# A two-layer graph network on one Trainium2 core: the f2 row sent in 4-byte pieces, set-up in finer steps, new step lists

## The chip, the cores and the metric

The kernel runs on 1 core of one Trainium2 chip. The metric is the device time in microseconds (us) of one execution. The engines are named as the profile names them: PE (TensorE matmuls), PEld (its weight loads), DVE (VectorE), ACT (ScalarE), POOL (GpSimd), SP (SyncE, which only issues DMAs). Each works through its own instruction list in order; lists meet at semaphores.

## The reference

The input x has 16 batch entries of 512 nodes with 256 features; adj is one 512 x 512 matrix of 0 and 1, the same for all entries. Cut to what matters:

```
h   = relu(layernorm(x))
# four attention heads, each with its own W (256x256) and a (2x256)
Wh  = h @ W;  f1 = Wh @ a[:256];  f2 = Wh @ a[256:]
e   = leaky_relu(f1[:, None] + f2[None, :], 0.01);  e = where(adj > 0, e, -1e9)
head = elu(softmax(e) @ Wh)
# a fifth head ("BACK") over the four heads side by side (1024 -> 256), then
y   = relu(out @ w1 + b1) @ w2 + b2 + out
x   = x + layernorm(y) * gamma + beta
h   = relu(layernorm(x))
x   = x + deg * (h @ Wi.T + b) + adj @ (h @ Wj.T)
```

For every head the score matrix needs f1 as one number per row and f2 as one number per column. f2 comes out of the product with one value per partition and has to be laid along the free axis of all 128 partitions.

## The kernel before, in words

Products that need precision are made of three matmuls on a split of each operand into a high and a low part (`product`, L775 to L785): ACT writes the high part, DVE the low part. The 512 nodes are 4 tiles of 128 (NC = 4). A batch entry has 10 **units**: a head times a half u of the rows (two tiles). Units 0 and 1 are head 0, 2 and 3 head 1, 4 and 5 the BACK head of an entry, 6 to 9 heads 2 and 3.

A unit goes through these steps, each on one engine: `rowmax` (DVE, L665: f2bc + mask, and its row maximum), `rowmath` (DVE, L679), `args` (ACT, L470: Prelu with f1 as bias, then Exp with the row sum), `rinv` and `scale` (DVE, L693 and L697), `turn_p` (PE, L844: 8 transposes), `probs` (ACT L482, DVE L688: high and low part), `attend` (PE, L854: 24 matmuls), `elu_neg`, `elu_exp` (ACT), `elu_out` (DVE), `hx` (ACT) and `hx_lo` (POOL). Around them stand per entry `norm_in`, `turn_in`, eight `m1` (12 matmuls each), four `mix2` (the BACK head's product, 24 matmuls each), `turn_out`, `ffn1`, `ffn2`, `norm_ff`, `x2`, `norm_gc`, `turn_gc`, two `conv_in`, `conv` and the store.

**The order of the work.** Each engine has a list of (step, index, late), `SP_STEPS` to `POOL_STEPS`. `steps` (L277) goes round the list; in round t it does the step for entry t - late, if there is one. So entries overlap: the attention of one entry, the feed-forward part of the one before and the convolution of the one before that run in one round. Steps named in `ONCE` (L275) are done for the first entry alone: they are set-up. An engine never skips a step that waits.

**PSUM** is four pairs of banks (`pairs`). PE's steps take them strictly in turn (L287 to L297): a PE step first waits until the pair's last user has been read (`take`, `lend`).

**How f2 gets to all partitions before.** `m1` ends on DVE with a copy of 4 columns out of PSUM (L663), f1 and f2 of two tiles; the BACK head's is in DVE's `mix2` (L718). Then PE's `f2turn` (L831) transposes the 128 x 4 column block into PSUM, ACT's `f2turn` (L463) copies the 4 x 128 result to `f2row`, SP's `f2send` (L337) writes it as 4 runs of 512 bytes to a row in DRAM scratch, and SP's `f2bcast` (L345) reads that row into all 128 partitions of one of two `f2bc` buffers. `rowmax` waits for it. It happens 5 times an entry, 80 times in all.

**Set-up before.** SP issues x of entry 0, then the head weights, a_heads, adj, W_gc, w1, w2 and the small vectors (L319 to L330). DVE starts with `norm_in` of entry 0 (L630), `wh_prep` of head 0 (L562), and `turn_in` (L654), and then alternates. `mask_` (L578) handles all four tiles at once, with a reduce on DVE. `load_wo` on SP (L361) brings W_out, a_out, b_gc and b2 in once `s_pick` and `s_wh` are there, since they go into buffers that set-up frees. `wo_prep` on DVE (L596) is one block of 5 + 16 + 3 operations. `adj_cast` (L617) and `adj_turn` (L623) are DVE's.

The opening of two lists, with entry numbers as b0, b1:

```
PE  turn_in.b0 m1(0,0) m1(0,1) m1(1,0) f2turn0 m1(1,1) gc_turn f2turn1 m1(2,0) m1(2,1)
    turn_p0 m1(3,0) turn_p1 attend0 m1(3,1) turn_p2 f2turn2 attend1 turn_in.b1 ...
DVE norm_in.b0 norm_in_out wh_prep0 turn_in.b0 wh_prep1 m1(0,0) wh_prep2 m1(0,1) mask m1(1,0)
    wh_prep3 m1(1,1) norm_in.b1 rowmax0 rowmath0 gc_turn rowmax1 rowmath1 rinv0 norm_in_out.b1
    scale0 m1(2,0) rowmax2 rowmath2 rowmax3 rinv1 m1(2,1) scale1 probs0 rowmath3 wo_prep ...
```

Of the kernel before, what the change touches and what calls it, by code (L numbers as in the profile page):

```python
# [21 lines left out]
ACT_STEPS = [
    ("hx", 0, 3), ("probs", 2, 3), ("f2turn", 2, 3), ("elu_neg", 1, 3), ("elu_exp", 1, 3), ("turn_in", 0, 2),
    ("turn_gc", 0, 5), ("args", 4, 4), ("elu_neg", 2, 3), ("elu_exp", 2, 3), ("f2turn", 3, 3), ("probs", 3, 3),
    ("args", 5, 4), ("conv_in", 0, 5), ("probs", 4, 4), ("hx", 1, 3), ("m1", (0, 0), 2), ("args", 6, 3), ("hx", 2, 3),
    ("conv_in", 1, 5), ("m1", (0, 1), 2), ("wh_prep", 0, 0), ("elu_neg", 3, 3), ("elu_exp", 3, 3), ("probs", 5, 4),
    ("elu_neg", 4, 4), ("wh_prep", 2, 1), ("elu_exp", 4, 4), ("probs", 6, 3), ("hx", 3, 3), ("m1", (1, 0), 2),
    ("args", 7, 3), ("f2turn", 0, 2), ("elu_neg", 5, 4), ("elu_exp", 5, 4), ("args", 8, 3), ("elu_neg", 6, 3),
    ("elu_exp", 6, 3), ("turn_out", 0, 4), ("probs", 7, 3), ("hx", 6, 3), ("m1", (1, 1), 2), ("probs", 8, 3), ("args", 9, 3),
    ("ffn1", 0, 4), ("elu_neg", 7, 3), ("elu_exp", 7, 3), ("hx", 7, 3), ("elu_neg", 8, 3), ("gc_turn", 0, 2),  # L30
    ("elu_exp", 8, 3), ("probs", 9, 3), ("f2turn", 1, 2), ("args", 0, 2), ("m1", (2, 0), 2), ("hx", 8, 3), ("args", 1, 2),
    ("elu_neg", 9, 3), ("elu_exp", 9, 3), ("m1", (2, 1), 2), ("probs", 0, 2), ("hx", 9, 3), ("wo_prep", 0, 2),
    ("norm_ff_out", 0, 4), ("norm_in_out", 0, 1), ("args", 2, 2), ("mix2", 0, 3), ("args", 3, 2), ("mix2", 1, 3),
    ("m1", (3, 0), 2), ("f2turn", -1, 3), ("probs", 1, 2), ("wh_prep", 1, 0), ("norm_gc_out", 0, 4), ("elu_neg", 0, 2),
    ("elu_exp", 0, 2), ("m1", (3, 1), 2), ("wh_prep", 3, 1),
]
# [945 lines left out]
```

## Time and profile before

| what | value |
|---|---|
| median of 3 runs | 1413.06 us (1412.38 to 1413.7) |
| the profiled execution's own time | 1413.76 us |
| its span in the trace | 1412.0 us |
| mean granted TensorE clock | 0.981 |
| PE busy | 1318.9 us, 93% of the span |
| DVE, ACT busy | 1097.5 us (78%), 1109.4 us (79%) |
| POOL busy | 346.7 us (25%) |

A busy share is the time in which an engine had an instruction running; starts of matmuls on PE lie closer together than their durations, because they are pipelined, so what a PE step takes is read from the distance of starts. The granted clock is TensorE's: 1.0 is 2.4 GHz, 0.5 is 1.2 GHz. The profiled execution is 0.7 us above the median.

### The profile page before, as it was taken

What the parts mean: (1) busy time and instruction counts of PE and PEld (TensorE: products, weight loads), DVE (VectorE), ACT (ScalarE), POOL (GpSimd) and SP (SyncE); (2) the same over time, 40 slices, a digit from 0 to 9 for tenths busy, and PEclk for the clock granted to TensorE, in tenths of its full rate; (3) what the DMA queues carried; (4) which work ended last, traced back from release to release, by engine and by line L of the source; (5) the groups of instructions that cost most, each with busy time, mean ns of one, the idle gap of its engine ahead of it and who ended that gap; (6) DMA issues with size and microseconds to landing.
All of it is one profiled execution on the core that took longest, in us unless ns stands there. A gap on an engine that the chain in (4) does not pass through costs nothing.

```text
span 1412.0 us, 27480 instructions
## 1 busy us (share of the span) xinstructions
PE 1318.9 (93%) x10024; PEld 1248.7 (88%) x10024; DVE 1097.5 (78%) x2841; ACT 1109.4 (79%) x2123; POOL 346.7 (25%) x234
## 2 busy tenths in 40 slices
PE   3689999999999999999999999999999999999874
PEld 3689898999999899999989999998999999899763
DVE  6997888787878878787887878788787878778442
ACT  3688987888888788887878878788887878888531
POOL 0021322314122231412223141222314122231411
PEclk9799999999999999999999999999999999999997
DMA  4211001011110101111020111102001110101000
...
DMA packets 42741, 55.14 MB, mean 39 GB/s; under 512 B 2864, under 2 KB 30832, under 8 KB 42480
## 3 DMA queue, kind: packets, MB, share of 16 engines
...
q14 instruction: 52, 0.43, 0.1%
...
## 4 chain that ended last, share of the span: by engine, by line
PE 66%; DVE 17%; ACT 11%; issue 6%; DMA 1%; POOL 0%; POOLq 0%; SPq 0%; ACTq 0%
PE ps L781 45%; PE ps L850 6%; PE ps L950 5%; PE ps L914 4%; PE ps L902 4%; DVE arg L701 3%; DVE arg L675 3%; ACT arg L479 2%; ACT elu L499 2%; DVE prob_lo L652 2%; DVE xb L742 2%; ACT arg L475 1%; DVE h2T_lo L652 1%; DVE zneg L683 1%; ACT prob_hi L485 1%
## 5 line engine op out<-in xcount | busy, mean ns | idle before, releaser
L398 POOL TENSOR_TENSOR hx_lo<-elu,hx_hi 128x512 fp32r<-128x512 f32 x128 | 177.3, 1385 | 867.2 <-ACT hx_hi L508 867.2
L781 PE MATMUL ps<-prob_hi,whx_hi 128*128 128x256 f32 x1024 | 301.6, 295 | 3.6 <-DVE prob_lo L652 3.6
L781 PE MATMUL ps<-prob_hi,whx_lo 128*128 128x256 f32 x1024 | 291.2, 284 | 0.0
L781 PE MATMUL ps<-prob_lo,whx_hi 128*128 128x256 f32 x1024 | 291.0, 284 | 0.0
L499 ACT ACTIVATE elu<-ps 128x512 f32<-128x512 f32 x160 | 94.4, 590 | 174.3 <-PE ps L781 174.3
L479 ACT ACTIVATE arg<-arg,nmax 128x512 f32<-128x512 f32 x320 | 226.6, 711 | 3.9 <-DVE nmax L686 3.8
L475 ACT ACTIVATE arg<-arg,fcol 128x512 f32<-128x512 f32 x320 | 211.9, 712 | 3.1 <-DVE gmax L675 3.1
L675 DVE CUSTOM_DVE_ANT_0 arg<-f2bc,mask 128x512 f32<-128x512 f32 x320 | 207.2, 684 | 5.4 <-DMA f2bc<-f_rows 5.4
L652 DVE TENSOR_TENSOR prob_lo<-ps,prob_hi 128x1024 fp32r<-128x1024 f32 x160 | 195.1, 1219 | 19.4 <-ACT prob_hi L485 17.8
L781 PEld LDWEIGHTS ps<-prob_hi,whx_hi 128*128 128x128 f32 x1024 | 197.5, 193 | 10.6 <-issue 5.9
L781 PEld LDWEIGHTS ps<-prob_hi,whx_lo 128*128 128x128 f32 x1024 | 197.6, 193 | 3.7 <-issue 3.6
L781 PEld LDWEIGHTS ps<-prob_lo,whx_hi 128*128 128x128 f32 x1024 | 197.6, 193 | 0.0
L850 PE MATMUL ps<-ident,arg 128*128 128x128 f32 x1280 | 167.3, 274 | 13.5 <-DVE arg L701 11.9
L711 DVE SCALAR_TENSOR_TENSOR elu<-elu,ps 128x512 f32<-128x512 f32 x128 | 87.7, 685 | 113.7 <-ACT elu L503 111.3
L701 DVE TENSOR_SCALAR arg<-arg,rinv 128x512 f32<-128x512 f32 x320 | 164.6, 556 | 2.4
L485 ACT ACTIVATE prob_hi<-ps 128x1024 fp32r<-128x1024 f32 x160 | 162.0, 1012 | 1.4 <-PE ps L850 1.4
L850 PEld LDWEIGHTS ps<-ident,arg 128*128 128x128 f32 x1280 | 144.8, 142 | 16.0 <-DVE arg L701 13.6
L781 PE MATMUL ps<-wh_hi,hT_hi 128*128 128x258 f32 x512 | 153.3, 299 | 2.5 <-DVE hT_lo L652 2.5
L781 PE MATMUL ps<-wh_lo,hT_hi 128*128 128x258 f32 x512 | 146.3, 286 | 0.0
L781 PE MATMUL ps<-wo_hi,hx_hi 128*128 128x258 f32 x512 | 146.0, 285 | 0.0
L781 PE MATMUL ps<-wh_hi,hT_lo 128*128 128x258 f32 x512 | 145.9, 285 | 0.0
L781 PE MATMUL ps<-wo_lo,hx_hi 128*128 128x258 f32 x512 | 144.9, 283 | 0.0
...
## 6 DMA issues: line engine op xcount, KB each, us to landing
f2bc<-f_rows SPq DMA_DIRECT2D x80, 256.0 KB, 3.2
...
f_rows<-f2row SPq DMA_DIRECT2D x80, 2.0 KB
...
```

Source lines behind the costliest of these rows:

```text
L398: pool.tensor_tensor(out=hx[1][:, 2 * c.h:2 * c.h + 2, c.u * HN:(c.u + 1) * HN], in0=elu[:, c.buf, :, :], in1=hx[0][:, 2 * c.h:2 * c.h + 2 ...
L475: act.activation(a[:, n, :], a[:, n, :], ACT.Prelu, bias=f1[:, n:n + 1], alpha=SLOPE).then_inc(arg_lin, 1)
L479: i = act.activation(a[:, n, :], a[:, n, :], ACT.Exp, bias=nmax[:, c.abuf, n:n + 1], accum_out=rsum[:, c.abuf, n:n + 1])
L485: act.activation(prob[0][:, c.buf, :, :].rearrange("p j i -> p (j i)"), pairs[c.pair][:, :, :].rearrange("p a n -> p (a n)"), ACT.Copy).th ...
L499: act.activation(elu[:, c.buf, :, :], pairs[c.pair][:, :, 0:F], ACT.Relu, scale=-1.0).then_inc(elu_neg, 1)
L652: return dve.tensor_tensor(out=dst, in0=src, in1=hi.bitcast(fp32), op=ALU.subtract)
L675: dve.tensor_tensor_reduce(out=arg[:, c.abuf, n, :], in0=f2bc[:, head % F2S, :], in1=mask[:, 2 * c.u + n, :], scale=1.0, scalar=-3.0e38, o ...
L701: i = dve.tensor_scalar(arg[:, c.abuf, n, :], arg[:, c.abuf, n, :], rinv[:, c.abuf, n:n + 1], None, ALU.mult)
L711: dve.scalar_tensor_tensor(out=dst, in0=elu[:, c.buf, :, :], scalar=-1.0, in1=pairs[c.pair][:, :, 0:F], op0=ALU.add, op1=ALU.max).then_inc ...
L781: i = pe.matmul(out, a, b_, start=(k == 0), stop=(k == n - 1))
L850: i = pe.transpose(p[:, j, n, :], arg[:, c.abuf, n, j * P:(j + 1) * P], ident[:, :])
L950: i = pe.matmul(pairs[c.pair][:, n // 2, (n % 2) * F:(n % 2 + 1) * F], adjT[:, j, n * P:(n + 1) * P], mj, start=(j == 0 and s == 0), stop= ...
```

## The change

f2 goes straight from its columns to the scratch row: `f2send` now reads the 128 x 4 column block and writes each element to its place, 512 pieces of 4 bytes. PE's and ACT's `f2turn` and the buffer `f2row` are gone.

```diff
             def f2send(c):
-                head = unit_number[c.b, c.info, 0] // 2
-                sp.wait_ge(f2_row, head + 1)
+                h = c.info
+                head = unit_number[c.b, h, 0] // 2
+                if h == BACK:
+                    sp.wait_ge(m2_read, 2 * (c.b + 1))
+                    column = fcol2[:, 1, :]
+                else:
+                    sp.wait_ge(m1_read, 2 * H * c.b + 2 * h + 2)
+                    column = fcol[:, h, 1, :]
                 if head >= 4:
                     sp.wait_ge(f2_spread[(head - 4) % F2S], 16 * ((head - 4) // F2S + 1))
-                sp.dma_start(f2_rows[head % 4].rearrange("(c q) -> c q", c=NC), f2row[:, :]).then_inc(f2_out[head % 4], 16)
+                sp.dma_start(f2_rows[head % 4].rearrange("(c q) -> q c", c=NC), column, allow_slow_non_contiguous=True).then_inc(f2_out[head % 4], 16)
...
-            def f2row_(c):
-                head = unit_number[c.b, c.info, 0] // 2
-                act.wait_ge(f2_turned, head + 1)
...
-            def f2turn(c):
...
-                take(c.pair)
-                pe.transpose(pairs[c.pair][0:NC, 0, 0:P], column, ident[:, :]).then_inc(f2_turned, 1)
-                lend((c.pair,), (f2_row, head + 1))
```

Set-up is cut finer. `wh_prep` on DVE leaves the low part of the weights to a step `wh_low`. `mask` works on two tiles at a time; its row sums move to ACT (`mask_` there, with accumulate), and a step `mask_end` finishes them. `adj_cast` (with the sums for deg) and `adj_turn` move from DVE to ACT. The b_gc part of `wo_prep` becomes `brow`; the rest becomes eight steps, one for each 128 rows of W_out:

```diff
+            def wh_low(c):
+                h = c.info
+                dve.wait_ge(s_wh_hi, h + 1)
+                for k in range(KC):
+                    i = dve.tensor_tensor(out=wh[1][:, k, h, 0:F], in0=w_heads[k][:, h, :], in1=wh[0][:, k, h, 0:F].bitcast(fp32), op=ALU.subtract)
+                i.then_inc(s_wh_lo, 1)
...
+            def mask_end(c):
+                dve.wait_ge(s_counted, c.info + 1)
...
+                i.then_inc(s_mask[c.info], 1)
+                if c.info == 0:
+                    dve.wait_ge(s_const, 3)
+                    dve.tensor_copy(pick[:, :], pick_st).then_inc(s_pick, 1)
...
+            def wo_prep(c):
+                k = c.info
                 for l in (LD_WO, LD_AO):
                     dve.wait_ge(ld[l], 16)
                 dve.wait_ge(s_gc_turned, 1)
...
+                for z in range(2):
+                    i = dve.tensor_tensor_reduce(out=xb[:, 2 * (k % 2) + z, :], in0=w_o[:, k, :], in1=a_o[:, z, :], scale=1.0, scalar=0.0,
+                                                 op0=ALU.mult, op1=ALU.add, accum_out=wsum2[:, k, z:z + 1])
+                link(i)
                 dve.wait_ge(s_wo_hi, 1)
+                link(dve.tensor_copy(wo[0][:, k, F:FA], wsum2[:, k, :]))
+                dve.tensor_tensor(out=wo[1][:, k, F:FA], ...)
+                dve.tensor_tensor(out=wo[1][:, k, 0:F], ...).then_inc(s_wo, 1)
...
             def load_wo(c):
                 sp.wait_ge(s_pick, 1)
+                sp.wait_ge(s_wh_lo, H)
                 sp.wait_ge(s_wh, H)
...
             def load_adj(c):
-                sp.wait_ge(s_wo, 1)
+                sp.wait_ge(s_wo, OC)
```

All five step lists are new, with `late` values up to 8. One round of three of them in the middle of the run, from `attend` of unit 5 on (numbers are units; b is the entry of heads 0 to 3, others are earlier ones):

```
PE  attend5 turn_p7 attend6 turn_p8 turn_out m1(2,0) attend7 ffn1 m1(2,1) turn_p9 attend8 m1(3,0)
    attend9 ffn2 mix2_0 mix2_1 turn_p0 mix2_2 mix2_3 turn_p1 m1(3,1) turn_in attend0 turn_p2
    attend1 turn_p3 turn_gc m1(0,0) attend2 m1(0,1) conv_in0 conv_in1 turn_p4 attend3 conv
    m1(1,0) turn_p5 attend4 turn_p6 m1(1,1)
ACT ... args2 mix2_1 probs1 m1(3,1) args3 turn_in elu0 probs2 norm_gc_out elu_neg1 hx0 elu_exp1
    turn_gc probs3 hx1 m1(0,0) elu2 args4 conv_in0 ...
SP  load f2bcast(-1) f2send3 f2bcast2 f2bcast3 store f2send0 f2send1 f2bcast0 load_back f2bcast1
    f2send(-1) f2send2
```

In the list of before PE did `conv_in` 1 after two more steps (m1(0,0), turn_p4) and `conv` after attend5 and adj_turn. The opening of the new lists:

```
PE  gc_turn turn_in.b0 m1(0,0) m1(0,1) m1(1,0) m1(1,1) m1(2,0) m1(2,1) adj_turn0 m1(3,0)
    adj_turn1 turn_p0 turn_p1 m1(3,1) turn_in.b1 attend0 turn_p2 attend1 turn_p3 ...
DVE wh_low0 wh_low1 wh_low2 wh_prep0 wh_prep1 wh_prep2 wh_low3 mask0 wh_prep3 mask_end0
    norm_in.b0 mask1 norm_in_out gc_turn brow wo_prep0 turn_in.b0 wo_prep1 wo_prep2 m1(0,0)
    wo_prep3 m1(0,1) wo_prep4 wo_prep5 wo_prep6 wo_prep7 norm_in.b1 m1(1,0) m1(1,1)
    norm_in_out.b1 mask_end1 rowmax0 m1(2,0) ...
SP  load_wo load.b1 f2send0 load_adj f2send1 f2bcast0 f2bcast1 f2send2 ...
```

In the last two entries PE's list ends `turn_gc.b14 conv_in0.b14 conv_in1.b14 turn_p4.b15 conv.b14 turn_p5.b15 attend4.b15 attend5.b15 turn_out.b15 ffn1 ffn2 turn_gc conv_in0 conv_in1 conv`; before it was `turn_gc.b14 conv_in0.b14 turn_p4.b15 conv_in1.b14 turn_p5.b15 attend4.b15 attend5.b15 conv.b14 turn_out.b15` and then the same.

## Rows read from the trace of the kernel before

**Rows 1.** The page, first part: busy time, share of span, instructions.

```profile
PE 1318.9 (93%) x10024; PEld 1248.7 (88%) x10024; DVE 1097.5 (78%) x2841; ACT 1109.4 (79%) x2123; POOL 346.7 (25%) x234
```

**Rows 2.** Busy time by stretch, two entries in mid-run; columns PE PEld DVE ACT POOL, clock.

```profile
345.00:516.00 171.00, 168.10 (x1303) 160.05 (x1302) 137.51 (x354) 143.47 (x275) 46.82 (x30) 1.00 0.11 35
```

**Rows 3.** Waits of PE, whole run: total us, times, longest.

```profile
PE ps L950 <- DVE prob_lo L652: 11.3, 13, 0.9
...
PE ps L781 <- DVE xb L742: 7.5, 13, 0.6
```

**Rows 4.** The chain that ended last: the same piece in two rounds running.

```profile
509.04 12.97 PE ps L781 x108
...
591.51 12.97 PE ps L781 x108
```

**Rows 5.** Timeline of PE, 527 to 542 us; start, duration, instruction.

```profile
527.13 1.04 PE L850 MATMUL ps<-ident,arg 128*128 128x128 f32 x8
...
528.19 0.36 PE L781 MATMUL ps<-prob_hi,whx_hi 128*128 128x256 f32 x1
...
535.74 0.27 PE L841 MATMUL ps<-ident,fcol 128*4 128x128 f32 x1
535.85 1.03 PE L850 MATMUL ps<-ident,arg 128*128 128x128 f32 x8
...
541.20 1.04 PE L850 MATMUL ps<-ident,arg 128*128 128x128 f32 x8
541.99 0.48 PE L781 MATMUL ps<-wg_hi,h2T_hi 128*128 128x512 f32 x1
```

**Rows 6.** Timeline of ACT: starts, from which the distance between steps is read.

```profile
46.16 2.06 ACT L446 ACTIVATE xin<-xin,shift_in,rstd_in 128x256 f32<-128x256 f32 x4
48.13 1.32 ACT L475 ACTIVATE arg<-arg,fcol 128x512 f32<-128x512 f32 x2
...
97.66 0.59 ACT L499 ACTIVATE elu<-ps 128x512 f32<-128x512 f32 x1
...
98.81 1.01 ACT L485 ACTIVATE prob_hi<-ps 128x1024 fp32r<-128x1024 f32 x1
...
99.88 1.32 ACT L475 ACTIVATE arg<-arg,fcol 128x512 f32<-128x512 f32 x2
...
102.52 0.57 ACT L461 ACTIVATE whx_hi<-ps 128x512 fp32r<-128x512 f32 x1
```

**Rows 7.** Waits of SP's DMA queue, whole run: total us, times, longest.

```profile
SPq L349 <- DMA f_rows<-f2row: 99.6, 78, 3.3
```

**Rows 8.** DMA issues (size, us to landing) and the packets of 0 to 12 us.

```profile
f2bc<-f_rows SPq DMA_DIRECT2D x80, 256.0 KB, 3.2
...
wk<-in_L_gnn_b SPq DMA_DIRECT2D x1, 128.0 KB, 7.5
...
b1c<-in_L_gnn_b SPq DMA_DIRECT2D x1, 1.0 KB, 10.5
...
DMA packets 2201, 3.59 MB, mean 299 GB/s; under 512 B 65, under 2 KB 1601, under 8 KB 2073
```

**Rows 9.** Timeline of the set-up: PE, DVE and SP rows.

```profile
10.47 0.43 DVE L559 CUSTOM_DVE_ANT_0 arg<-wk,ff 128x256 f32<-128x256 f32 x1 [2.22 <-DMA ff<-in_L_gnn_a_heads]
...
16.30 0.55 PE L781 MATMUL ps<-wh_hi,hT_hi 128*128 128x258 f32 x1 [2.46 <-DVE hT_lo L652]
...
37.41 0.99 SPq L367 DMA_DIRECT2D wk<-in_L_gnn_b  x1
...
47.69 0.28 DVE L599 CAST w2x_hi<-wk 128x256 fp32r<-128x256 f32 x1
...
49.70 0.43 DVE L608 CUSTOM_DVE_ANT_0 xb<-ff,wk 128x256 f32<-128x256 f32 x1
```

**Rows 10.** Timeline of the end: conv of entry 14 and turn_out behind it.

```profile
1358.62 0.28 PE L950 MATMUL ps<-h2T_hi,adjT 128*128 128x256 f32 x1
...
1362.46 1.04 PE L888 MATMUL ps<-ident,wk 128*128 128x128 f32 x8
```

More of the change, by code:

```diff
@@ L21 @@
+    ("attend", 3, 5), ("conv", 0, 7), ("m1", (1, 0), 4), ("turn_p", 5, 6), ("attend", 4, 6), ("turn_p", 6, 5),
+    ("m1", (1, 1), 4),
 ]
 ACT_STEPS = [
[L23 to L35, printed above, removed]
+    ("conv_in", 0, 8), ("m1", (0, 1), 5), ("conv_in", 1, 8), ("args", 5, 7), ("wh_prep", 2, 2), ("wh_prep", 3, 3),
@@ L36 @@
+    ("turn_gc", 0, 7), ("probs", 3, 5), ("hx", 1, 5), ("m1", (0, 0), 4), ("wh_prep", 1, 1), ("elu_neg", 2, 5),
+    ("elu_exp", 2, 5), ("args", 4, 6),
 ]
 DVE_STEPS = [
-    ("elu_out", 3, 4), ("probs", 5, 5), ("elu_out", 4, 5), ("mask", 0, 3), ("rowmax", 8, 4), ("rowmath", 7, 4),
-    ("rowmath", 8, 4), ("probs", 6, 4), ("m1", (1, 0), 3), ("rowmax", 9, 4), ("rinv", 7, 4), ("elu_out", 5, 5),
-    ("scale", 7, 4), ("adj_turn", 0, 4), ("rowmath", 9, 4), ("wh_prep", 3, 3), ("rinv", 8, 4), ("conv", 0, 6),
@@ new lines @@
+    ("rowmax", 3, 6), ("gc_turn", 0, 5), ("mix2", 1, 7), ("rinv", 2, 6), ("norm_gc", 0, 8), ("rowmath", 3, 6),
+    ("scale", 2, 6), ("probs", 1, 6), ("m1", (3, 1), 6), ("wh_low", 3, 3), ("brow", 0, 5), ("norm_gc_out", 0, 8),
+    ("rinv", 3, 6), ("scale", 3, 6), ("wo_prep", 0, 5), ("turn_in", 0, 5), ("wo_prep", 1, 5), ("elu_out", 0, 6),
+    ("probs", 2, 6), ("elu_out", 1, 6), ("wo_prep", 2, 5), ("turn_gc", 0, 8), ("probs", 3, 6), ("m1", (0, 0), 5),
+    ("rowmax", 4, 7), ("rowmath", 4, 7), ("mask_end", 0, 4), ("rowmax", 5, 7), ("rowmax", 6, 6), ("wo_prep", 3, 5),
@@ new lines @@
+    ("mask", 0, 3), ("wh_low", 0, 1), ("rowmath", 5, 7), ("rinv", 4, 7), ("scale", 4, 7), ("wh_low", 1, 1),
+    ("rowmath", 6, 6), ("elu_out", 2, 6), ("m1", (0, 1), 5), ("conv_in", 0, 8), ("conv_in", 1, 8), ("wo_prep", 4, 5),
+    ("wo_prep", 5, 5), ("rowmax", 7, 6), ("wo_prep", 6, 5), ("rowmath", 7, 6), ("rinv", 5, 7), ("probs", 4, 7),
+    ("scale", 5, 7), ("wo_prep", 7, 5), ("norm_in", 0, 4), ("rinv", 6, 6), ("elu_out", 3, 6), ("conv", 0, 8),
+    ("scale", 6, 6), ("wh_low", 2, 1), ("m1", (1, 0), 5), ("probs", 5, 7), ("rowmax", 8, 6), ("rinv", 7, 6),
@@ L59 @@
+    ("norm_gc", 0, 6),
 ]
@@ L254, in gnn_kernel @@
                       "elu_out", "hx", "hx_lo")
-        IN_PSUM = ("turn_in", "m1", "f2turn", "turn_p", "attend", "mix2", "turn_out", "ffn1", "ffn2", "turn_gc", "conv_in", "conv", "gc_turn", "adj_turn")
+        IN_PSUM = ("turn_in", "m1", "turn_p", "attend", "mix2", "turn_out", "ffn1", "ffn2", "turn_gc", "conv_in", "conv", "gc_turn", "adj_turn")
         STEPS = {"SP": SP_STEPS, "PE": PE_STEPS, "ACT": ACT_STEPS, "DVE": DVE_STEPS, "POOL": POOL_STEPS}
@@ L272, in gnn_kernel @@
             pass
-        ONCE = ("load_wo", "load_adj", "wh_prep", "mask", "gc_turn", "wo_prep", "adj_cast", "adj_turn")
+        ONCE = ("load_wo", "load_adj", "wh_low", "wh_prep", "mask", "mask_end", "gc_turn", "brow", "wo_prep", "adj_cast", "adj_turn")
         def steps(table):
@@ L584, in mask_ @@
[L584 to L590 removed]
+                tiles = slice(2 * c.info, 2 * c.info + 2)
```

162 lines of the change are left out of this document (79 added, 83 removed), and 9 rows, old and new, of tables (PE_STEPS, SP_STEPS).

## The prediction

> **What bounds the kernel now.** I read the page's busy line first, then a mid-run stretch, then PE's waits, then the two ends. PE is busy 93% of the span, and no other engine is above 79% [rows 1]. In mid-run, 171 us hold 168.1 us of PE at full clock [rows 2]: PE is the bound there, and what a step costs is its slot on PE plus any wait in front of it. The same piece of the chain returns after 591.51 - 509.04 = 82.47 us [rows 4], the time of one round, so of one entry. PE idles (171 - 168.1) x 82.47 / 171 = 1.4 us of it [rows 2], and two waits fill that: one before `conv` (L950), 11.3 us in 13, and one before the second `conv_in` (until DVE's L742), 7.5 us in 13 [rows 3]. The `conv` wait is put down to prob_lo at L652, a helper's line; its true releaser is DVE's low part of conv_in. A bare round is thus 82.47 - 1.4 = 81.1 us of PE work.
>
> PE's other idle time, 1412.0 - 1318.9 = 93 us in all [rows 1], less the 18.8 us of these two waits [rows 3] and a few of their like, lies in the first 174 us and the last 80. There latencies and DVE's set-up decide, not PE.
>
> **Part 1: f2turn leaves PE.** What it takes is the distance of starts, not its 0.27 us of duration. Between products and a turn_p, it moves turn_p by 535.85 - 535.74 = 0.11 us. After a turn_p, the next product starts 528.19 - 527.13 = 1.06 us after turn_p's start with an f2turn between, and 541.99 - 541.20 = 0.79 us without: 0.27 us [rows 5]. Of the five in that round I read four at 0.11 to 0.12 and one at 0.27, so 0.72 us a round, and 16 x 0.72 = **-11.5 us**. All of it lies on PE, the bound, so it counts in full.
>
> ACT loses a short copy (a slot of about 0.16 us) five times a round. ACT is 79% busy [rows 1], PE never waits for that copy in mid-run, and it counts zero by itself. PSUM has 5 fewer users a round, so every pair comes round a little later relative to the work; I count nothing.
>
> **Part 2: the new order in mid-run.** I laid PE's new list out back to back (m1 1.44, attend 2.86, turn_p 0.88, mix2 2.87, conv_in 3.0, conv 4.1 us from starts in the trace) and followed ACT's and DVE's lists beside it.
> - The two old waits go. conv now stands behind both conv_in, a turn_p and an attend: 3.7 us pass between the end of conv_in 1 and conv, against about 1.2 us that ACT and DVE need for its low part. conv_in 1 takes the pair that m1(0,0) held, read some 4 us earlier. **-18.8 us** [rows 3].
> - New close places appear, above all `turn_gc`, behind ACT's norm_gc_out. From the end of m1(3,1) to turn_gc PE has turn_in, attend0, turn_p2, attend1, turn_p3 = 0.88 + 2.86 + 0.88 + 2.86 + 0.88 = 8.4 us. ACT has m1 0.5, args 102.52 - 99.88 = 2.64, turn_in about 0.9, elu 98.81 - 97.66 = 1.15, probs 0.9, norm_gc_out 48.13 - 46.16 = 1.97, together 8.1 us [rows 6]. That leaves 0.3 us for all semaphore delays. With ACT's durations (1.32 for a pair, 2.06 for the norm [rows 6]) instead of distances, it comes about 1.0 us late. Just behind it attend2 needs unit 1's elu_out, which waits for the same ACT run. So new waits lie between 0 and 1.0 us a round, hardly below 0, since there is nothing left to remove. I take 0.3 us, near the end made of distances, because an in-order engine that always has work runs at distances: 15 rounds, **+4.5 us**.
>
> **Part 3: the send in 512 pieces.** No DMA of 4-byte pieces from the chip's side to DRAM is in the trace. From below it is the old send of 4 runs, for whose landing SP waited 99.6 / 78 = 1.3 us [rows 7]. From above it is b1c, 256 pieces of 4 bytes, 10.5 us [rows 8], but issued behind more than 4 MB of loads. Nearer is a bound by packets: in 12 us 16 engines handled 2201 packets, so a packet costs at most 16 x 12 / 2201 = 0.087 us of an engine [rows 8]. 512 pieces on 16 engines are 32 each, at most 2.8 us more. I take 3.0 us to landing. A saving stands against it: no PE turn and ACT copy in front, about 0.45 us.
>
> Is it hidden? In mid-run, yes: the tightest is head 0. f2bcast0 stands behind f2send1, which waits for m1(1,1) to be read; I find its issue 6.5 us before DVE reaches rowmax0. The broadcast needs 3.2 us [rows 8], leaving **3.3 us** of cover, and it queues behind the pieces of f2send1 (at most 2.8 us). The BACK head and head 3 have 3 to 6 us. SP's other waits (store, load, load_back, each now between sends) are over before the sends' conditions hold. The cost in mid-run is zero, and the cover is thin.
>
> The packet count above prices a piece like any other packet. A rule speaks against the change here. The Trainium skill, page "DMA: Bandwidth & Descriptors", sections "Specifications" and "Rules for kernel authors", says that a non-contiguous last dimension becomes one descriptor per element and should be rearranged, and that transfers below 512 B are read-modify-write. No row here shows a write that small; if the rule bites, the third rival below is what it does.
>
> **Part 4: the set-up.** PE's first product starts at 16.30 us, behind DVE's turn_in [rows 9]. In the new list DVE does all of wh_prep, wh_low, half the mask, norm_in, brow and wo_prep0 before turn_in. Walking it: wh_low 0 to 2 until a_heads lands at 10.5 [rows 9]; four wh_prep of about 1.8 us (four dots and two small steps), wh_low3 0.7, mask0 1.3 and mask_end0 1.0 bring s_pick at about 20.9. Only then does SP issue load_wo; in the old run b_gc was issued 1.05 us after the first of these transfers, at 37.41, and takes 7.5 us [rows 8, 9], so it is there at 29.4. brow takes 49.70 - 47.69 = 2.0 us [rows 9], wo_prep0 1.5, turn_in 1.2: **first product at about 34.2 us, 17.9 us later than before.**
>
> Much of that comes back, since DVE's later set-up is gone: the 10.6 us block of wo_prep that left PE 6.5 us idle is spread, and 8.4 us of reduce, cast and copies went to ACT. Followed on, attend0 ends at about 67.5 us with both adj_turn and turn_in of entry 1 done. PE work behind it at full speed is then 20.7 us, so 46.8 us are lost; in the old run 49.8 us are lost at 99.9 us and about 52 at 174. I find 7 more lost until 100 us in the new order (scale6 comes 2.9 us late, scale7 and scale8 about 1 each) and about 2 for the low clock after a gap, and 1 or 2 for later sends. That is 57 or 58 against 52: **+6 us**. Both ends: all of the 17.9 remains, or the finer steps pay and it is -5.
>
> **Part 5: the end.** After the last mix2 the BACK head's f2 is on the path, with nothing beside it. Send and turn: 3.0 - 1.3 - 0.45 = about +1.3 us [rows 7]. And conv of entry 14, 1362.46 - 1358.62 = 3.8 us [rows 10], used to run after the last attend, mostly beside the elu; now it stands before turn_p5 and both last attends, and I find turn_out 2.5 us later. **+4 us** (0 to 8).
>
> **Sum**, against the profiled execution's own 1413.76 us: -11.5 - 18.8 + 4.5 + 6 + 4 = -15.8, so **1398 us**. The median of the runs shown is 0.7 us lower, which I leave in the range. A measurement of this kernel can tell about 0.2%, 2.8 us, from no change.
>
> **The rivals.**
> - *New waits as large as the old* (14%). The slips behind norm_gc_out and elu_out reach 1.0 us a round with small ones at other places, 1.4 us together: 1398 + 15 x 1.1 = 1414.5. For: the 0.3 us of spare. Against: ACT idles just before that run, and waits for attends.
> - *The start is not regained* (14%). PE starts 17.9 us late, and the later gaps do not shrink: 1398 - 6 + 17.9 = 1410. For: the wait for load_wo stands before everything. Against: the walk, in which the set-up after it is lighter.
> - *The pieces arrive late* (12%), the one that ends slower. Place: f2bcast0 behind f2send1's pieces, in front of rowmax0. It decides from 3.3 us of pieces on. At b1c's 10.5 us [rows 8] the broadcast lands 6.7 us after DVE wants it; scale9 then comes 3.1 us after PE wants turn_p9, and DVE's idle stretch before m1(3,0) takes up the rest. 15 x 3.1 = 47: 1445. At 5 us it would cost little. For: no row bounds a 4-byte write to DRAM from above but b1c's. Against: the packet bound of part 3. The rule of the Trainium skill cited there, page "DMA: Bandwidth & Descriptors", would lead here.
> - *The row holds other data, so the change does other work*: piece (q, c) goes to c x 128 + q, where the old turn put it. None.
>
> **How the numbers follow.** The forecast has 60%; its own range is 1389 to 1407 (start and end each off by 5 or so, new waits 0 to 0.7 a round). With the first two rivals the range is 1385 to 1415, and the third is left outside. Faster: the forecast, half of the first rival and most of the second, 0.76; same 0.12; slower 0.12.
>
> **What the changed profile would show.** A round of 80.5 to 80.8 us in the chain instead of 82.47; no waits at conv and conv_in; a small one at turn_gc or the attend behind it. The first product near 34 us. f2 sends landing in about 3 us and no mid-run DVE wait at rowmax. It is wrong if the round is above 81.5, if rowmax waits for f2bc in mid-run, or if PE has lost much over 58 us by the time the rounds are regular.

## The result, and the profile after

The changed kernel takes 1517.45 us (median of 4 runs, 1515.31 to 1523.14) against 1413.38 us for the kernel before in the same session: ratio 1.0743, 95% interval 1.0712 to 1.0774. It is **104 us slower** where 15 us less were forecast, and outside the range. The profiled execution has a span of 1514.7 us.

The page of the changed kernel, busy line, packets, queue q1 and the chain by engine and by line (lines of the file have moved: the product L781 is L810, turn_p L850 is L867, rowmax L675 is L701, the send is L352):

```profile
PE 1339.3 (88%) x9944; PEld 1267.4 (84%) x9944; DVE 1101.7 (73%) x2859; ACT 1103.4 (73%) x2063; POOL 339.5 (22%) x234
...
DMA packets 84339, 55.12 MB, mean 36 GB/s; under 512 B 44784, under 2 KB 72432, under 8 KB 84080
...
q1 hardware_dynamic: 84208, 53.39, 18.9%
...
PE 48%; DMA 24%; DVE 17%; issue 5%; ACT 5%; SPq 1%; POOL 0%; POOLq 0%; DVEq 0%; ACTq 0%
PE ps L810 30%; DMA f2bc<-f_rows 12%; DMA f_rows<-fcol 11%; PE ps L867 6%; DVE arg L701 4%; PE ps L967 4%; PE ps L931 4%; PE ps L919 3%; ACT arg L503 2%; DVE arg L727 2%; DVE nmax L712 2%; DVE prob_lo L678 1%; DVE elu L738 1%; DVE wk L750 1%; DVE xb L756 1%
```

All 80 f2turns are gone from PE (9944 instructions for 10024), and yet PE's busy share fell from 93% to 88% [rows 1]: PE now waits. A quarter of the chain is DMA, and both parts of it are f2's: the send into the row and the broadcast behind it.

Waits of SP's queue and of DVE in the changed kernel (total, times, longest):

```profile
SPq L358 <- DMA f_rows<-fcol: 371.9, 58, 12.1
```

```profile
DVE arg L701 <- DMA f2bc<-f_rows: 128.5, 43, 12.1
```

SP waited 1.3 us for a send to land before [rows 7]; it waits 6.4 us now, up to 12.1. And rowmax, which never waited for f2 in mid-run, waits 43 times.

The chain of the changed kernel in one mid-run round, and SP's timeline of the same stretch:

```profile
567.24 0.36 SPq L352
567.70 12.46 DMA f_rows<-fcol
580.23 10.12 DMA f2bc<-f_rows
590.37 0.69 DVE arg L701
```

```profile
567.24 0.91 SPq L352 DMA_DIRECT2D f_rows<-fcol  x2
568.21 0.50 SPq L338 DMA_DIRECT2D xin<-in_x  x1
577.15 0.33 SPq L359 DMA_DIRECT2D f2bc<-f_rows  x1
577.58 0.39 SPq L352 DMA_DIRECT2D f_rows<-fcol  x1
580.23 10.32 SPq L359 DMA_DIRECT2D f2bc<-f_rows  x2
```

Two sends go out at 567.24; the first broadcast leaves at 577.15, the second at 580.23, 12.5 us behind its send. Between them a third send went into the same queue at 577.58, and the broadcast of 580.23 takes 10.1 us to land where the usual one took 3.2 [rows 8]. So a slow send seems to cost twice: before its own broadcast, and in front of another head's. The DMA engines aren't short of time while this goes on. Their busy share in tenths and what they moved, 560 to 600 us in slices of 1 us:

```profile
DMA  0000000041102354425599930000000184000000
GB/s 0 0 0 0 0 0 0 0 4 25 41 0 11 37 29 32 18 34 16 95 235 169 188 146 0 0 0 0 0 0 0 14 156 92 0 16 0 0 0 0
```

The last packets end at 584, and the broadcast counts as landed at 590.35: for 6.3 us nothing moves. What the landing waits for in that time, the trace doesn't name; that the third send's pieces are it is my reading. By the store of the result, a round is 517.34 to 605.61 and 605.61 to 692.57 us, 88.3 and 87.0 us, for 82.47 before [rows 4]. The stretch 345 to 516 us of the changed kernel, columns as in [rows 2]:

```profile
345.00:516.00 171.00, 161.02 (x1216) 153.21 (x1215) 131.54 (x337) 134.21 (x253) 42.68 (x28) 0.97 0.22 34
```

1216 PE instructions fit in it for 1303 [rows 2]. PE idles 10 us instead of 3, and after such a gap part of the stretch ran below the upper clock level of 2.4 GHz: in 500 to 505 us PE was busy for 1.6 us, and in 505 to 510 the granted clock was 0.50 (0.97 over the whole stretch, for 1.00 before).

### The profile page after: what moved, and what is told of

It reads as the page before. It is cut to its first block, busy times and chain, and to the rows that moved or that the text cites. A ratio compares the mean times of both kernels' runs of the same rounds, so it can differ in the third digit from the quotient of the medians.

```text
span 1514.7 us, 27134 instructions
## 1 busy us (share of the span) xinstructions
PE 1339.3 (88%) x9944; PEld 1267.4 (84%) x9944; DVE 1101.7 (73%) x2859; ACT 1103.4 (73%) x2063; POOL 339.5 (22%) x234
## 2 busy tenths in 40 slices
DMA packets 84339, 55.12 MB, mean 36 GB/s; under 512 B 44784, under 2 KB 72432, under 8 KB 84080
## 4 chain that ended last, share of the span: by engine, by line
PE 48%; DMA 24%; DVE 17%; issue 5%; ACT 5%; SPq 1%; POOL 0%; POOLq 0%; DVEq 0%; ACTq 0%
PE ps L810 30%; DMA f2bc<-f_rows 12%; DMA f_rows<-fcol 11%; PE ps L867 6%; DVE arg L701 4%; PE ps L967 4%; PE ps L931 4%; PE ps L919 3%; ACT arg L503 2%; DVE arg L727 2%; DVE nmax L712 2%; DVE prob_lo L678 1%; DVE elu L738 1%; DVE wk L750 1%; DVE xb L756 1%
## 5 line engine op out<-in xcount | busy, mean ns | idle before, releaser
L408 POOL TENSOR_TENSOR hx_lo<-elu,hx_hi 128x512 fp32r<-128x512 f32 x128 | 167.0, 1305 | 849.4 <-ACT hx_hi L533 789.2
L810 PE MATMUL ps<-prob_hi,whx_hi 128*128 128x256 f32 x1024 | 306.8, 300 | 1.6 <-DVE elu L738 1.1
L701 DVE CUSTOM_DVE_ANT_0 arg<-f2bc,mask 128x512 f32<-128x512 f32 x320 | 208.6, 690 | 134.5 <-DMA f2bc<-f_rows 128.5
L810 PE MATMUL ps<-prob_hi,whx_lo 128*128 128x256 f32 x1024 | 298.7, 292 | 0.0
L810 PE MATMUL ps<-prob_lo,whx_hi 128*128 128x256 f32 x1024 | 297.8, 291 | 0.0
L867 PE MATMUL ps<-ident,arg 128*128 128x128 f32 x1280 | 180.3, 287 | 90.7 <-DVE elu L738 50.1
L867 PEld LDWEIGHTS ps<-ident,arg 128*128 128x128 f32 x1280 | 153.2, 148 | 102.0 <-DVE arg L727 88.8
L810 PEld LDWEIGHTS ps<-prob_hi,whx_hi 128*128 128x128 f32 x1024 | 206.6, 202 | 2.9 <-issue 2.0
L810 PEld LDWEIGHTS ps<-prob_hi,whx_lo 128*128 128x128 f32 x1024 | 206.3, 202 | 0.0
L810 PEld LDWEIGHTS ps<-prob_lo,whx_hi 128*128 128x128 f32 x1024 | 205.5, 201 | 0.0
L810 PE MATMUL ps<-wh_hi,hT_hi 128*128 128x258 f32 x512 | 157.4, 307 | 3.4 <-DVE hT_lo L678 2.6
L727 DVE TENSOR_SCALAR arg<-arg,rinv 128x512 f32<-128x512 f32 x320 | 154.1, 523 | 2.4
L810 PE MATMUL ps<-wo_hi,hx_hi 128*128 128x258 f32 x512 | 148.4, 290 | 0.0
L810 PE MATMUL ps<-wh_lo,hT_hi 128*128 128x258 f32 x512 | 146.5, 286 | 0.0
L810 PE MATMUL ps<-wh_hi,hT_lo 128*128 128x258 f32 x512 | 146.3, 286 | 0.0
L810 PE MATMUL ps<-wo_lo,hx_hi 128*128 128x258 f32 x512 | 144.5, 282 | 0.0
L810 PE MATMUL ps<-wo_hi,hx_lo 128*128 128x258 f32 x512 | 144.3, 282 | 0.0
L678 DVE TENSOR_TENSOR whx_lo<-ps,whx_hi 128x512 fp32r<-128x512 f32 x128 | 87.6, 685 | 69.5 <-ACT whx_hi L492 69.1
```

Of the source, the lines that this page charges most:

```text
L408: pool.tensor_tensor(out=hx[1][:, 2 * c.h:2 * c.h + 2, c.u * HN:(c.u + 1) * HN], in0=elu[:, c.buf, :, :], in1=hx[0][:, 2 * c.h:2 * c.h + 2 ...
L678: return dve.tensor_tensor(out=dst, in0=src, in1=hi.bitcast(fp32), op=ALU.subtract)
L701: dve.tensor_tensor_reduce(out=arg[:, c.abuf, n, :], in0=f2bc[:, head % F2S, :], in1=mask[:, 2 * c.u + n, :], scale=1.0, scalar=-3.0e38, o ...
L727: i = dve.tensor_scalar(arg[:, c.abuf, n, :], arg[:, c.abuf, n, :], rinv[:, c.abuf, n:n + 1], None, ALU.mult)
L810: i = pe.matmul(out, a, b_, start=(k == 0), stop=(k == n - 1))
L867: i = pe.transpose(p[:, j, n, :], arg[:, c.abuf, n, j * P:(j + 1) * P], ident[:, :])
```

## The experiments

**What the parts cost: sends of 4-byte pieces in the old order, and the new order without them.** e1 puts only the send (and the loss of f2turn) into the kernel before; the step lists and the set-up stay old. e2 and e5 take f2 out of the sum: a row of zeros goes out in four runs of 512 B, in the new and in the old order.

```
e1: before, without the f2turn steps, and
-   sp.dma_start(f2_rows[k].rearrange("(c q) -> c q", c=NC), f2row[:, :])
+   sp.dma_start(f2_rows[k].rearrange("(c q) -> q c", c=NC), column, allow_slow...)
e2: after, e5: e1, each with
+   pool.memset(f2row[:, :], 0.0)
-   sp.dma_start(f2_rows[k].rearrange("(c q) -> q c", c=NC), column, allow_slow...)
+   sp.dma_start(f2_rows[k].rearrange("(c q) -> c q", c=NC), f2row[:, :])
```

> The kernel before with one part of the change alone: f2 is sent in 512 pieces of 4 bytes, f2turn is gone from PE and ACT, the step lists and the set-up are the old ones. Theory A (the pieces are slow: in the changed trace a send is on the chain for 12.5 us and the broadcast behind it for 10.1) expects the old order to suffer as well, since rowmax of head 0 and of the BACK head stand no further from their sends there: rounds of 85 us or more and 1450 to 1520 us. Theory B (the new lists and the late set-up cost the time, the pieces little) expects 1402 us: 1413.4 less the 11.5 us of PE's f2turn.

> The changed kernel with new lists and new set-up, but each send writes a fixed row of zeros in 4 runs of 512 bytes, under the same waits (the f2 values are left out, so the attention scores are others; no instruction of the engines changes). Theory A expects the forecast of the new lists without the slow pieces: a round of 80.4 to 81 us and 1390 to 1402 us. Theory B expects it to stay above 1480 us.

> The kernel before with its own lists and set-up, f2turn gone, and the fixed row of zeros sent in 4 runs (the f2 values are left out). This measures part 1 of the prediction alone, the slots that f2turn has on PE: 1413.4 - 11.5 = 1402 us by both theories, a round of 81.75 us in place of 82.47. If it is over 1410, the slots that f2turn leaves turn into waits.

Measured: e1 1625.12 us (ratio 1.15, 1.1431 to 1.1569), e2 1406.87 us (0.995, 0.9933 to 0.9966), e5 1387.10 us (0.9813, 0.9798 to 0.9827). The whole loss is the 4-byte send: 110.6 us in the new order (after less e2), 238 us in the old (e1 less e5). The new order covers part of the landing; it does not make it. e1 came out 105 us above the top of what I had expected of slow pieces. By its stores, a round is 80.61 us in e5 and 80.84 in e2.

```profile
500.46 12.98 PE ps L781 x108
...
581.08 12.97 PE ps L781 x108
```

That fence is e5's chain. e5 was a miss to the good side: 26.8 us off for 11.5. PE's waits in e5:

```profile
PE ps L781 <- DVE xb L742: 6.0, 13, 0.5
```

The wait of conv_in is still there (7.5 before [rows 3]), the one of conv (11.3 us in 13) is gone. No list changed here but for the missing f2turns, so that wait went with f2turn itself. The lists say how. PE's steps take the four PSUM pairs in turn. In the kernel before, the order up to conv is turn_p6, m1(1,0), f2turn0, attend5, conv, so conv gets the pair of turn_p6, which is free only once DVE has written unit 6's low part, prob_lo; that is the releaser that the profile names:

```profile
560.29 0.36 PE L950 MATMUL ps<-h2T_hi,adjT 128*128 128x256 f32 x1 [0.87 <-DVE prob_lo L652]
```

That prob_lo runs from 558.93 to 560.15 us. Without f2turn0, conv gets the pair of attend4, one step further back.

PE's matmuls by stretch (start, middle, end; the third window reaches past the end of the program, and an instruction that crosses a bound is counted on both sides), of before, e5 and e2 in this order:

```profile
0.00:174.00 174.00, 133.48 (x993) 127.82 (x994) 143.70 (x404) 126.47 (x245) 28.00 (x29) 0.93 0.23 73
174.00:1200.00 1026.00, 1008.62 (x7796) 959.58 (x7795) 827.95 (x2137) 857.43 (x1647) 270.43 (x175) 1.00 0.12 36
1200.00:1515.00 315.00, 176.78 (x1239) 161.30 (x1237) 125.87 (x304) 125.54 (x234) 48.27 (x30) 0.95 0.06 18
```

```profile
0.00:174.00 174.00, 132.80 (x992) 127.10 (x993) 144.87 (x405) 125.94 (x235) 29.27 (x31) 0.92 0.23 73
174.00:1200.00 1026.00, 1020.00 (x7910) 975.06 (x7909) 844.36 (x2185) 868.24 (x1621) 277.31 (x178) 1.00 0.12 36
1200.00:1515.00 315.00, 150.90 (x1047) 136.96 (x1046) 104.82 (x254) 104.61 (x188) 44.12 (x27) 0.95 0.06 17
```

```profile
0.00:174.00 174.00, 127.30 (x964) 122.52 (x965) 136.40 (x421) 127.98 (x248) 26.04 (x29) 0.95 0.22 74
174.00:1200.00 1026.00, 1015.10 (x7871) 969.82 (x7870) 863.01 (x2162) 858.15 (x1609) 268.44 (x178) 1.00 0.12 36
1200.00:1515.00 315.00, 164.93 (x1114) 146.88 (x1112) 117.67 (x277) 113.91 (x207) 44.72 (x28) 0.93 0.05 17
```

The f2turns of before in the same stretches, 11, 63 and 6 at the end:

```profile
0.00:174.00 174.00, 3.24 (x11) 0.95 (x11) 0.93 0.23 73
174.00:1200.00 1026.00, 17.11 (x63) 5.19 (x63) 1.00 0.12 36
1200.00:1412.00 212.00, 1.63 (x6) 0.49 (x6) 0.93 0.09 27
```

Take them out of before's counts and divide by 7871 / 1026 = 7.67 matmuls per us. Against before, e2 is 18 matmuls or 2.3 us behind at 174, does 138 more or 18.0 us in the middle, and has 119 (1114 for 1233) or 15.5 us less left at 1200, but takes 205.5 us for it where before took 212.0: 9.0 us more than its share. Together -6.7 us, and the spans differ by -6.5. For e5 the same gives -1.3, -23.1 and -2.3. So the new lists and set-up, once the pieces are away, cost 20 us against the old ones: 3.6 at the start, 5.1 in the middle, and 11.3 in the last 200 us.

**Larger pieces.** e3 sends 128 runs of 16 B in the new order; the row then lies in the order (q c), and rowmax reads it with a step of 4 elements. e6 and e9 lay the mask out in the same order, once, in the set-up, so that rowmax reads without a step, and turn_p picks every fourth column of the scores (old order and new).

```
-   f2_rows[k].rearrange("(c q) -> q c", c=NC)
+   f2_rows[k].rearrange("(q c) -> q c", c=NC)
e3: rowmax reads f2bc[...].rearrange("p (q c) -> p c q", c=NC)
e6, e9: the mask is written as mask[:, n, :].rearrange("p (q c) -> p c q", c=NC), and
-   pe.transpose(p[:, j, n, :], arg[..., j * P:(j + 1) * P], ident)
+   pe.transpose(p[:, j, n, :], arg[...].rearrange("p (q c) -> p c q", c=NC)[:, j, :], ident)
```

> The changed kernel, but f2 goes out as one run of 16 bytes for each partition (128 pieces in place of 512), and rowmax reads the broadcast row with a step of 4 elements. Theory A with a cost per piece expects the send's landing to fall from about 10 us to a third, 3 to 4 us, and 1395 to 1410 us. Theory A with a cost that hangs on the write's being under 512 bytes and not on the count expects about the time of the change, 1500 us. Theory B expects 1480 us or more. If the strided read slows rowmax (0.61 us a tile now), DVE's row shows it.

> Old lists and set-up, f2turn gone, f2 sent as 128 runs of 16 bytes, and the whole score row kept in the order the runs lie in: the mask is written in that order once, rowmax reads everything with step 1, and turn_p on PE picks every fourth column. If PE's transposes read a step of 4 elements at their old distance (0.11 us each), it comes to the time of e5, 1387 us (1386 to 1391), and beats both kernels. If the strided read slows a transpose by 0.1 us, 80 of them a round add 8 us a round and it is near 1510.

> The changed kernel with new lists and new set-up, and with e6's send of 16-byte runs, permuted mask and strided turn_p. If the pieces' size is all that separates the change from e2, it ends at 1405 to 1410, 108 us under the change, and stays about 20 us above e6, the cost of the new lists. If it lies above 1420, the new lists leave less cover for the send than a landing of 1.9 us needs.

Measured: e3 1492.08 us (1.0554, 1.0538 to 1.0569), e6 1398.26 us (0.9897, 0.988 to 0.9913), e9 1418.59 us (1.0037, 1.0022 to 1.0052). The row of rowmax in e3:

```profile
L701 DVE CUSTOM_DVE_ANT_0 arg<-f2bc,mask 128x512 f32<-128x512 f32 x320 | 357.6, 1159 | 3.3 <-DMA f2bc<-f_rows 2.6
```

The pieces no longer hold rowmax up (2.6 us of waiting in the whole run; a send lands in 1.9 us), but rowmax takes 1.16 us for 0.68, 20 times a round, and VectorE becomes the bound: it has 49% of the chain, for 17% in the changed kernel. The time alone, 1492 us, would have fitted the reading that size and not number is slow; the landing of 1.9 us rules that out for 16 bytes. e6 avoids that and **beats both kernels**: 15 us under before with the reference's computation whole. By the ratios it keeps 14.6 of e5's 26.4 us. In the page of before and of e6, the weight loads of turn_p:

```profile
L850 PEld LDWEIGHTS ps<-ident,arg 128*128 128x128 f32 x1280 | 144.8, 142 | 16.0 <-DVE arg L701 13.6
```

```profile
L836 PEld LDWEIGHTS ps<-ident,arg 128*128 128x128 f32 x1280 | 167.9, 209 | 19.4 <-DVE arg L700 18.1
```

The scores are the stationary operand here. Loading them with a step takes 209 ns for 142, and the distance from turn_p's start to the next step grows from about 0.79 to 0.88 us, ten times a round; a round of e6 is 81.22 us for e5's 80.61. The expectation had neither a free stride (1387) nor one of 0.1 us a transpose (1510) right: it costs about 0.01 us each. e9 less e6 is 20.3 us, again the price of the new lists and set-up, though e9 itself lies 9 us above the range I gave.

**Is it the number of pieces, their size, or where they go?** From here on the broadcast reads a row of zeros (f2 is left out of all or most of the scores), the lists are old, and only the send changes. e7 sends one column, 128 pieces of 4 B side by side, for the 512.

```
e7:  f2_rows[k][0:P] <- column[:, 0:1]                      (128 pieces, step 4 B)
e10: f2_wide[k, 0:16 * P], every 16th <- column[:, 0:1]     (128 pieces, step 64 B)
e11: f2_wide[k], every 16th <- column                       (512 pieces, step 64 B)
e12: f2_wide[k, 0:4 * P], every 4th <- column[:, 0:1]       (128 pieces, step 16 B)
e13: f2_wide[k, 0:P] <- column[:, 0:1]                      (128 pieces, step 4 B)
e14: f2_wide[k, 0:N] <- column                              (512 pieces, step 4 B)
e15: f2_rows[k], every 4th <- column[:, 0:1]                (128 pieces, step 16 B)
```

f2_rows is what the broadcast reads; f2_wide is read by nothing.

> As e5 (old lists, no f2turn), but a send writes 128 pieces of 4 bytes, one for each partition (a quarter of the f2 values, the rest of the row stays zero). It tells what makes the 4-byte send slow. If every 4-byte piece has its own price, 10.3 us for 32 pieces an engine becomes (10.3 - 1.3) / 4 + 1.3 = 3.5 us to landing for 8 an engine, and the kernel ends at 1390 to 1405. If a piece of 4 bytes costs what one of 16 costs, it lands in 1.9 us as e3's send did, and the kernel ends at 1387 to 1389.

> e7 (old order, the broadcast reads a fixed row of zeros, f2 is left out of the scores, 128 pieces of 4 bytes are written for each head), but each of the 128 pieces goes to a place of its own, 64 bytes from the next, in a scratch that nothing reads, where in e7 the 128 pieces lay side by side. Only the addresses differ. Theory C, pieces that are written side by side into the same 64 bytes wait for each other (16 of them per 64 bytes in e1 and e7, 4 in e6): the wait for the send falls from 8.15 us to under 3 us and the run takes 1387 to 1400 us, as e5 and e6. Rival D, a piece of 4 bytes is slow by its size, wherever it goes: the wait stays at 8 us and the run at 1590 to 1610 us.

> The same with all 512 pieces of 4 bytes of a head, each 64 bytes from the next (the broadcast still reads a fixed row of zeros, so f2 is left out). Theory C: with no two pieces in the same 64 bytes the number alone is left; 512 pieces by the 0.087 us and 16 engines of the prediction are 2.8 us, and the run takes 1387 to 1410 us. Rival D: at least as long as e7, 1590 us or more (e1, with 512 side by side, took 1625).

> e10 with the 128 pieces of 4 bytes 16 bytes apart, so that 4 of them share 64 bytes, as the pieces of 16 bytes do in e6 (the broadcast reads a fixed row of zeros, so f2 is left out). Theory C: as e6, a wait of 2.7 us for the send and 1390 to 1405 us. Rival D: as e7 and e10, 1590 to 1610 us.

> e7 with its 128 pieces of 4 bytes side by side, but in a scratch that nothing reads, as in e10 and e12 (the broadcast reads a fixed row of zeros elsewhere, so f2 is left out). e10 to e12 changed two things against e7: the spacing, and that the row written is not the row that the broadcast reads. This changes the second alone. Theory C (pieces side by side wait for each other): as e7, a wait for the send of 8 us and 1590 to 1610 us. Rival E (a row of small pieces is slow because it is also read, by the broadcasts): a wait under 3 us and 1387 to 1400 us.

> The same with all 512 pieces of 4 bytes side by side in the scratch that nothing reads (f2 is left out). Theory C: as e1, a wait of 9 us and 1600 to 1640 us. Rival E: as e11, 1387 to 1410 us.

> e12's 128 pieces of 4 bytes at 16 bytes apart, but written into the row that the broadcast reads, as in e7 (the other three quarters of the row stay zero, so f2 is left out of most of the scores). Theory C: spacing decides, so as e12, a wait of 2.5 us and 1387 to 1400 us. Rival E: the reading decides, so as e7, a wait of 8 us and 1590 to 1610 us.

| run | pieces, step | row read? | us | ratio, 95% interval | SP waits for the send, us each |
|---|---|---|---|---|---|
| e5 | 4 of 512 B | yes | 1387.10 | 0.9813, 0.9798 to 0.9827 | 1.7 |
| e1 | 512, 4 B | yes | 1625.12 | 1.15, 1.1431 to 1.1569 | 9.1 |
| e7 | 128, 4 B | yes | 1602.42 | 1.1332, 1.129 to 1.1373 | 8.2 |
| e13 | 128, 4 B | no | 1514.84 | 1.072, 1.0685 to 1.0755 | 7.2 |
| e14 | 512, 4 B | no | 1639.45 | 1.159, 1.1555 to 1.1625 | 8.5 |
| e12 | 128, 16 B | no | 1386.93 | 0.9814, 0.98 to 0.9829 | 2.4 |
| e15 | 128, 16 B | yes | 1387.71 | 0.9821, 0.9807 to 0.9836 | 2.6 |
| e10 | 128, 64 B | no | 1386.84 | 0.9812, 0.9796 to 0.9829 | 2.1 |
| e11 | 512, 64 B | no | 1387.69 | 0.9819, 0.9804 to 0.9833 | 2.5 |

The last column is the wait of SP's queue divided by its count. e7 missed both of its readings (1387 to 1405). e10 to e12 changed two things against e7, the step and whether the row is read; e13, e14 and e15 take these apart. e13 met neither of its readings (1387 to 1400, or 1590 to 1610): it lies between. Four of those rows, of e7, e13, e15 and e11:

```profile
SPq L355 <- DMA f_rows<-fcol: 635.8, 78, 10.6
```

```profile
SPq L356 <- DMA f_wide<-fcol: 551.4, 77, 9.3
```

```profile
SPq L355 <- DMA f_rows<-fcol: 203.8, 78, 5.1
```

```profile
SPq L356 <- DMA f_wide<-fcol: 194.7, 78, 4.6
```

And two sends with the broadcasts behind them, from SP's timelines of e7 and of e15:

```profile
551.72 0.45 SPq L349 DMA_DIRECT2D f_rows<-fcol  x1
560.08 0.33 SPq L356 DMA_DIRECT2D f2bc<-f_rows  x1
560.50 0.38 SPq L349 DMA_DIRECT2D f_rows<-fcol  x1
569.80 0.32 SPq L356 DMA_DIRECT2D f2bc<-f_rows  x1
```

```profile
513.74 0.32 SPq L349 DMA_DIRECT2D f_rows<-fcol  x1
515.18 0.32 SPq L356 DMA_DIRECT2D f2bc<-f_rows  x1
515.59 0.38 SPq L349 DMA_DIRECT2D f_rows<-fcol  x1
519.52 0.32 SPq L356 DMA_DIRECT2D f2bc<-f_rows  x1
```

e7 and e15 differ in nothing but the step of the addresses: a send holds its broadcast back 8.4 and 9.3 us at 4 B, 1.4 and 3.9 us at 16 B. The pieces are of one size and number, and the row is read in both. With the pieces apart, the number matters little (e10 and e11: 0.4 us for four times as many) and the size by itself nothing that shows in the time. Once they are side by side, both number and reading count, but not as a plain sum: unread, four times as many cost 125 us more (e14 less e13); with 128 pieces the reading costs 88 us (e7 less e13), with 512 none (e1 less e14: -14 us). How far the pieces spread in DRAM isn't it either: e12's 128 and e14's 512 both cover 2 KB, and only e14 is slow. **4-byte pieces written side by side are what lands slowly.** My theory's words, that those in the same 64 bytes wait for each other, go further than this: e12 and e15 put 4 pieces into 64 bytes and lose nothing, so all that is shown is that 4 B apart is slow and 16 B apart is not. Steps of 8 B, and in what unit the pieces meet, were not tried.

The packets themselves aren't slower. e14 and e11 have the same 84240 packets in the queue, which took 12.1% of 1642 us and 14.0% of 1386, so 199 and 194 us. The difference comes after them. e14's send of 562.35 holds its broadcast until 571.57, and the DMA engines are idle (share 0.00) from 566.3 on; e13's of 532.52 holds it until 539.59, and they are idle from 536.0 on; e12's of 560.64 holds it until 564.64, idle from 564.0. The last packet is followed by 5.3, 3.6 and 0.6 us of silence. What goes on in it no run shows.

**Where the new order loses at the end.** conv of an entry now stands in front of both last attends, and I took it for a part of the loss. e8 is e2 with conv put behind attend5 on PE and behind elu_out5 on DVE, and the store behind f2bcast0 on SP.

> As e2 (new lists, fixed row), but conv stands behind attend5 on PE and behind elu_out5 on DVE, and the store behind f2bcast0 on SP. It takes the cause of the late end apart. If conv in front of the last two attends is what makes the end late, turn_out of the last entry comes 2.3 us earlier, ffn1 runs at full clock again (3.1 us less), and the kernel comes to 1400 to 1403 from 1407. If the length of the lists' overlap is the cause, nothing changes at the end, 1405 to 1409.

Measured: 1429.31 us (1.0115, 1.0097 to 1.0134), 20 us or more above both readings. The move makes a wait of its own at turn_p:

```profile
PE ps L871 <- DVE arg L731: 32.8, 22, 5.4
```

In e2 that wait is 11.0 us in 9. e8's round is 82.33 us, which hides what the end gained. From the start of the last but one ffn2 to the end of the span it is 102.5 us in e2, 101.7 in e8 and 95.6 in e5. The 6.9 us between e2 and e5 can be placed. turn_out of the last entry comes 2.5 us later in e2 (counted from turn_gc), as the prediction had it, and ffn1 behind it takes twice as long for the same 8 matmuls, at a granted clock of 0.55 in 1355 to 1362 us, after PE had been busy for 1.9 us of the 5 before. In e2 and e5:

```profile
1355.07 6.77 PE L923 MATMUL ps<-ff,w_sb 128*128 128x512 f32 x8 [1.11 <-ACT ff L551]
1339.10 3.70 PE L889 MATMUL ps<-ff,w_sb 128*128 128x512 f32 x8 [1.11 <-ACT ff L522]
```

In e8 ffn1 takes 3.70 us again, as expected, but a wait of 5.4 us at turn_p takes it back: turn_out isn't 2.3 us earlier but 2.5 later. So 3.1 us of the end are the lower clock and 2.5 the later turn_out; the rest of the end's 9 us stays without a shown cause.

**The strided access, put elsewhere.** e16 is e6 with the step moved from turn_p's reading to rowmax's writing.

```
-   out=arg[:, c.abuf, n, :]
+   out=arg[:, c.abuf, n, :].rearrange("p (c q) -> p q c", c=NC)      (turn_p reads as in before)
```

> A version meant to beat e6: f2 in runs of 16 bytes and the mask laid out as in e6, so that rowmax reads both without a stride, but rowmax writes its result with a stride (element q of block c), so that the scores are in natural order again and turn_p reads them without a stride, as in before and e5. If a strided write costs rowmax nothing (0.69 us), the run takes 1387 to 1393 us, 6 to 10 below e6. If a strided write costs what e3's strided read did (1.16 us for 0.69, 20 instructions a round, 9 us of VectorE), VectorE is near its bound again: 1450 to 1490 us. Rival in between: the write is free, but what e6 lost was the shorter wait for the send and not turn_p's reading: then 1396 to 1400 us as e6.

Measured: 1515.59 us (1.072, 1.0705 to 1.0734), 26 us above the dearest reading. A strided write is at least as dear for VectorE as a strided read (1.25 us for 1.16); of the three places tried, the step is cheapest on PE.

```profile
L674 DVE CUSTOM_DVE_ANT_0 arg<-f2bc,mask 128x512 f32<-128x512 f32 x320 | 376.1, 1254 | 5.2 <-DMA f2bc<-f_rows 5.2
```

## Why the prediction was wrong

**Part 3 failed, and it alone turned the sign.** "A bound by packets" priced a piece at no more than 0.087 us of an engine and got at most 2.8 us over the old landing, and I took 3.0 to landing. As a price of the number of pieces the bound holds: e11's 512 pieces, 64 B apart, make SP wait 2.5 us for e5's 1.7. But the row it came from [rows 8] is of loads out of DRAM, and what decides is where small writes fall in it. The row could not show that, and the sentence "the packet count above prices a piece like any other packet" was where I should have left the forecast open. The upper bound I wrote down beside it, b1c's 10.5 us, was near the truth (6.4 us of waiting on average, up to 12.1; in e1 a send lands in 10.3 us by the median), and I chose the lower as nearest. That b1c came so close is luck: it is a load, issued behind others. And a bound by the engines' busy time could not see the cost at all, since most of it lies behind the last packet.

The rule quoted there, from the Trainium skill, page "DMA: Bandwidth & Descriptors", sections "Specifications" and "Rules for kernel authors", stood on the right side. Its count agrees: 44784 - 2864 more packets under 512 B are 524 a send, 512 and 12 others (e3, with 128 pieces, has 140). On size it gives no price, and size alone has none here: e10 to e12 and e15 write the same 4 bytes without loss. Whether a read-modify-write is behind the slow case, no run shows.

**The rival "the pieces arrive late" came in, at 1517 us and not 1445.** Its place was right (a late broadcast in front of rowmax), its size wrong by a factor of two. I let one head, f2bcast0, be late once a round, 3.1 us. The trace has 43 waits at rowmax in 16 entries, 128.5 us, and they chain: SP issues in order and waits for a send before the broadcast, the next send's pieces go in front of a broadcast (10.1 us to landing), and PE then runs part of the time at the lower clock level. The two rounds shown are longer than most; the 13 from 258.74 to 1387.44 us take 86.8 us each. Against e2 the round thus grew by 6.0 us, 16 x 6.0 = 96 of the 110.6 us that lie between the changed kernel and e2. Its chance of 12% was too small for a cost whose bounds were 1.3 and 10.5 us and whose cover was 3.3.

**Part 1 was too small.** e5 gains 26.8 us for 11.5. The slots of f2turn weren't measured by themselves, but with conv's 11.3 us and 1.5 at conv_in they make 24.3 of it. "PSUM has 5 fewer users a round ... I count nothing" is the term that was wrongly put at nothing: conv's wait [rows 3] went with f2turn, because conv then gets another pair. And "its true releaser is DVE's low part of conv_in" was a misreading: the profile's prob_lo is unit 6's, and it was the releaser.

**Part 2 was right in its sum and wrong in its credit.** The round was forecast at 80.5 to 80.8 us; e2, which has the new lists and no slow pieces, has 80.84. But old lists without f2turn do as well (80.61), so the reordering, to which I gave 18.8 us, brought nothing in mid-run that f2turn's removal hadn't. Of the new waits I named turn_gc; in e2 it is turn_p2, three steps before it, that waits. It takes the PSUM pair of turn_p1, which is free once unit 1's prob_lo is written: the same kind of wait as conv's before.

```profile
526.06 1.06 PE L871 MATMUL ps<-ident,arg 128*128 128x128 f32 x8 [0.82 <-DVE prob_lo L682]
```

It does so 14 times, 11.5 us, for my 4.5.

**Part 4 was near.** First product at 32.0 us for 34.2. By the count above the start costs 2.3 us against before, or 3.6 against e5, which has lost its f2turns too, for +6: the second rival, that the start is not regained, is out.

**Part 5 was too small.** +4 us, of which 2.7 without the pieces; by e2's count the end costs 9.0 us. The 2.5 us at turn_out were right; ffn1 at the lower clock level, 3.1 us, was no term of it.

Without the 4-byte pieces the forecast of 1398 would have met 1406.87: 9 us off, 6 of them at the end, and just inside the forecast's own range of 1389 to 1407. That is in part luck: in the middle, the gain that I credited to the lists came from f2turn's going, and the lists themselves cost 5 us there.
